# At most three indirect transfers in flight, in place of a wait for all at every fourth

## Time and profile before

| | us |
|---|---|
| median of three executions | 1523.4 |
| lowest, highest | 1520.61, 1532.26 |
| the profiled execution | 1523.45 |
| its span, first to last instruction | 1521.7 |
| PE busy (matmul) | 1223.2 (80% of the span) |
| DVE busy | 934.8 (61%) |
| POOL busy | 563.9 (37%) |
| ACT busy | 541.5 (36%) |

### The profile page before, as it was taken

The page is one execution under the profiler, slowest core; times in us unless marked ns, Lnnn a source line. Parts: engine busy times, 40 slices in busy tenths (PEclk is TensorE's granted clock), DMA queues, the critical chain, the costliest instruction groups (busy, mean ns, idle before and its releaser), DMA issues. The chain is left out here.

```text
span 1521.7 us, 31374 instructions
## 1 busy us (share of the span) xinstructions
PE 1223.2 (80%) x11687; PEld 1053.5 (69%) x11687; DVE 934.8 (61%) x2307; ACT 541.5 (36%) x1254; POOL 563.9 (37%) x645
## 2 busy tenths in 40 slices
PE   7999997895747999689985674858589999998920
PEld 4555557684747999689883453645589999988920
DVE  4777764788615644355544766575559777877732
ACT  3444431354605555244442331422323233222200
POOL 5000002000375656555205550055502555555655
PEclk9999998998558999899997785668579999999965
DMA  8600000004013333233214210011112333333341
GB/s 322 248 1 1 1 0 8 1 1 127 9 52 103 119 114 112 86 101 107 79 57 109 76 41 3 1 40 40 38 49 80 109 105 106 109 97 96 91 144 55
DMA packets 93251, 115.49 MB, mean 76 GB/s; under 512 B 18294, under 2 KB 77553, under 8 KB 93105
## 3 DMA queue, kind: packets, MB, share of 16 engines
q1 hardware_dynamic: 72144, 62.73, 13.4%
q0 software_dynamic: 20960, 50.76, 10.4%
HBM read 53.01 MB, written 60.42 MB: 75 GB/s over the span
## 5 line engine op out<-in xcount | busy, mean ns | idle before, releaser
L1393 POOL DMA_INDIRECT sorted_rows<-s_normed,s_places x128 | 130.8, 1022 | 211.5 <-DVE s_places L1359 120.8
L1554 PE MATMUL g_bank<-weights,gx_hT 128*128 x1360 | 169.8, 279 | 0.4 <-ACT gx_hT L1582 0.2
L1469 POOL DMA_INDIRECT sx_fetch<-sorted_results,s_places x128 | 132.7, 1037 | 99.9 <-DMA sx_fetch<-sorted_results,s_places 68.4
L1393 POOL DMA_INDIRECT sorted_rows<-g_normed,g_places x128 | 131.8, 1029 | 95.8 <-DMA sorted_rows<-g_normed,g_places 40.0
L1469 POOL DMA_INDIRECT gx_fetch<-sorted_results,g_places x128 | 126.0, 984 | 102.2 <-DMA gx_fetch<-sorted_results,g_places 70.8
L1554 PEld LDWEIGHTS g_bank<-weights,gx_hT 128*128 128x128 f32 x1360 | 162.7, 196 | 1.2 <-issue 1.2
L1517 PE MATMUL s_bank<-sx_xT_high,sx_w_now 128*128 128x256 f32 (+1 forms) x510 | 152.1, 298 | 1.8 <-DVE sx_hT L1629 1.2
L1518 PE MATMUL s_bank<-sx_xT_low,sx_w_now 128*128 128x256 f32 (+1 forms) x510 | 144.3, 283 | 0.0
L1519 PE MATMUL s_bank<-sx_xT_high,sx_w_now 128*128 128x256 f32 (+1 forms) x510 | 144.3, 283 | 0.0
L1554 PE MATMUL s_bank<-weights,sx_hT 128*128 (+1 forms) x1020 | 132.6, 280 | 5.4 <-issue 3.9
L1582 ACT ACTIVATE gx_hT<-g_bank,gx_b_now 128x256 f32<-128x256 f32 x340 | 132.8, 481 | 3.0 <-PE g_bank L1554 3.0
(11 more groups left out here) (434 smaller groups left out, 2757.6 us busy)
## 6 DMA issues: line engine op xcount, KB each, us to landing
sorted_rows<-zeros POOLq DMA_DIRECT2D x29, 512.0 KB, 15.5
gx_xq<-sorted_rows SPq DMA_DIRECT2D x85, 128.0 KB, 2.1
sorted_results<-gx_yq SPq DMA_DIRECT2D x85, 128.0 KB, 1.9
sx_xq<-sorted_rows SPq DMA_DIRECT2D x85, 128.0 KB, 2.1
sorted_results<-sx_yq SPq DMA_DIRECT2D x85, 128.0 KB, 2.2
feats<-in_x SPq DMA_DIRECT2D x8, 512.0 KB, 7.8
out<-tokens SPq DMA_DIRECT2D x16, 256.0 KB, 3.8
g_raw_up<-in_L_ffn_W SPq DMA_DIRECT2D x1, 2048.0 KB, 9.5
```

What stands on the lines that cost most here:

```text
L1393: pool.indirect_dma_start(out=sorted_rows[g], out_offset=bass.IndirectOffsetOnAxis(ap=places[:, at, r:r + 1], axis=0), in_=normed[:, at, : ...
L1469: pool.indirect_dma_start(out=fetch[n % 2][:, i, r, :], out_offset=None, in_=self.sorted_results[g], in_offset=bass.IndirectOffsetOnAxis(a ...
L1554: done = pe.matmul(down[u % 2][:, P * k:P * k + C], hT[u % 2][0:width, i, P * k:P * k + P], self.w_down[0:width, bass.ds(e, 1), i, :].rear ...
```

## The change

The waits at every fourth transfer go. In their place stands a class `Flight` with three semaphores that go round: transfer k of a stage counts on semaphore k mod 3, and before transfer k is issued POOL waits until transfer k - 3, the last on that semaphore, has landed. This holds for sends and fetches of both expert stages, the first group of the GELU stage included. Whoever needs a whole group or part (SP before the first unit of a group, DVE before the first tile of a part and at the start of the window attention) waits for the counts of all three semaphores in place of one. All other waits and the order of all work stay.

```diff
-def send_group(pool, plan, g, normed, places, sorted_rows, sent, pauses=True):
-    for at in range(plan.first_tile[g], plan.first_tile[g + 1]):
-        for r in range(2):
-            pool.indirect_dma_start(...).then_inc(sent[g], 16)
-        if at % 2 == 1 and pauses:
-            pool.wait_ge(sent[g], (at + 1 - plan.first_tile[g]) * 2 * 16)
+FLIGHT = 3
+class Flight:
+    def __init__(self, t, name):
+        self.slots = [t.sem(f"{name}{i}") for i in range(FLIGHT)]
+    def slot(self, k):
+        return self.slots[k % FLIGHT]
+    def wait_landed(self, engine, end):
+        for i, slot in enumerate(self.slots):
+            engine.wait_ge(slot, 16 * len(range(i, end, FLIGHT)))
+def send_group(pool, plan, g, normed, places, sorted_rows, sent):
+    for k in range(2 * plan.first_tile[g], 2 * plan.first_tile[g + 1]):
+        at, r = k // 2, k % 2
+        if k >= FLIGHT:
+            pool.wait_ge(sent.slot(k), k // FLIGHT * 16)
+        pool.indirect_dma_start(...).then_inc(sent.slot(k), 16)
...
                     for r in range(2):
+                        k = (n * SEND + i) * 2 + r
+                        if k >= FLIGHT:
+                            pool.wait_ge(fetched.slot(k), k // FLIGHT * 16)
                         pool.indirect_dma_start(
                             out=fetch[n % 2][:, i, r, :], out_offset=None, in_=self.sorted_results[g],
...
-                            ).then_inc(fetched[n % 2], 16)
-                    if i % 2 == 1:
-                        pool.wait_ge(fetched[n % 2], (n // 2 * SEND + i + 1) * 2 * 16)
+                            ).then_inc(fetched.slot(k), 16)
...
-                sp.wait_ge(self.sent[g], 2 * plan.tiles[g] * 16)
+                self.sent.wait_landed(sp, 2 * plan.first_tile[g + 1])
...
-            dve.wait_ge(self.fetched[part % 2], (part // 2 + 1) * 2 * SEND * 16)
+            self.fetched.wait_landed(dve, (part + 1) * 2 * SEND)
...
-                send_group(pool, plan, 0, normed, places, group_rows, sent, pauses=False)
+                send_group(pool, plan, 0, normed, places, group_rows, sent)
```

More of the change, by code:

```diff
@@ L1386, in place_in_pieces @@
         steps.settle()
-def send_group(pool, plan, g, normed, places, sorted_rows, sent, pauses=True):
-    for at in range(plan.first_tile[g], plan.first_tile[g + 1]):
-        for r in range(2):
-            pool.indirect_dma_start(
-                out=sorted_rows[g], out_offset=bass.IndirectOffsetOnAxis(ap=places[:, at, r:r + 1], axis=0),
-                in_=normed[:, at, :], in_offset=None).then_inc(sent[g], 16)
-        if at % 2 == 1 and pauses:
-            pool.wait_ge(sent[g], (at + 1 - plan.first_tile[g]) * 2 * 16)
+FLIGHT = 3
[12 more added lines that the diff above has]
+            pool.wait_ge(sent.slot(k), k // FLIGHT * 16)
+        pool.indirect_dma_start(
+            out=sorted_rows[g], out_offset=bass.IndirectOffsetOnAxis(ap=places[:, at, r:r + 1], axis=0),
+            in_=normed[:, at, :], in_offset=None).then_inc(sent.slot(k), 16)
 class Units:
@@ L1440, in __init__ @@
         self.alone = 0 if kind.gelu else 1
-        self.fetched = [t.sem(f"{tag}fetched{i}") for i in range(2)]
+        self.fetched = Flight(t, f"{tag}fetched")
         self.x_loaded = [t.sem(f"{tag}x_loaded{i}") for i in range(4)]
@@ L2208, in vector @@
         if units:
-            for g, n in enumerate(units.plan.tiles):
-                dve.wait_ge(units.sent[g], 2 * n * 16)
+            units.sent.wait_landed(dve, 2 * TT)
         normalise(0)
@@ L2245, in gelu_and_first_half @@
         normed = t.sbuf("g_normed", [P, TT, C])
-        sent = [t.sem(f"gx_sent{g}") for g in range(plan.groups)]
+        sent = Flight(t, "gx_sent")
         room = t.sbuf("g_room", [P, 4 * HALF])
@@ L2511, in silu_and_second_half @@
         normed = t.sbuf("s_normed", [P, TT, C])
-        sent = [t.sem(f"sx_sent{g}") for g in range(plan.groups)]
+        sent = Flight(t, "sx_sent")
         with ExitStack() as routing:
```

## The result

The changed kernel takes 1448.2 us (median; 1443.58 to 1451.21), the kernel before 1522.3 beside it: a ratio of 0.9505, 95% interval 0.9458 to 0.9551. Predicted were 1446 us. The profiled execution took 1451.2 us, with a span of 1449.5, 72.2 less than before.

| stretch (how measured) | before | after | gain so far | gain of the stretch | predicted |
|---|---|---|---|---|---|
| GELU group 0 (last send) | 455.28 | 455.13 | 0.15 | 0 | 0 |
| GELU units (POOL's clearing after all stores) | 797.09 | 763.62 | 33.5 | 33.5 | 33 |
| first window attention (POOL's first work behind it) | 938.25 | 896.89 | 41.4 | 7.9 | 11 |
| second window, SiLU units, end (last fetch) | 1513.87 | 1441.48 | 72.4 | 31.0 | 33 |

A forecast was written before the change was run, and what follows sets the result against it. The prediction took POOL's indirect transfers, idling until each burst of four landed, to bound the kernel from the SiLU stage on. Gains of 33 + 11 + 33 = 77 us against 1523.45 gave 1446, range 1436 to 1476.

The forecast's parts named there:

- Period: Spacing of POOL's transfers after the change: issue plus 0.30 us gap limits, not landings; 1.34 us, between 1.25 and 1.64.
- 4.5 at most: Longest landing time of a transfer in us, giving a third of landing plus resuming of 1.5 us at the worst.
- signs of a wrong forecast: DVE still waiting for fetches in units, POOL gaps for landings of k - 3, or issues over 1.04 us on average.
- GELU group 0 at nothing: First group's sends in the GELU stage, newly given waits: no loss at the nearest row, 11 us lost at the upper end.
- GELU units, 33: GELU stage units: SP's wait for group 2 and DVE's waits for fetches go, leaving 3.44 us a unit; 33 us less.
- up to p of about 1.9: In the GELU units, DVE was to have no waits for fetches while a transfer's period stayed below about 1.9 us.
- First window, 11: First window attention: most of DVE's 15.2 us of waiting for fetched parts goes; 11 us less, at worst 5, at best 15.
- SiLU units and end, 33: SiLU units to last fetch: stalls go, part 12 starts at 1439.4, last fetch starts 32.9 us earlier; 33 us less.
- Fetches stay late: Rival: POOL's wait for earlier adds replaces the removed one, DVE's 28.3 us of waits stay; time 1498, chance 0.08.
- Slower: Rival: three transfers in steady flight land later than bursts, at SP's GELU group 2 wait and last fetches; 1668, chance 0.05.
- no effect: Rival: landings hold POOL at its present pace throughout; time 1523, chance 0.03.
- DVE slows the issue: Rival: POOL's issues in the units meet DVE's 0.87 us weight copies, period 1.95 us; gain 20, time 1503, chance 0.05.

The follow-up runs named there:

- sends alone: Changed kernel with only the sends three in flight, fetches keeping the wait at every fourth transfer; 1498.3 us, ratio 0.9841 to the kernel before.
- free sends: Changed kernel with sends not waiting for landings at all, on one semaphore a group, fetches still three at a time; 1448.7 us, ratio 0.9542.
- copy on ACT and early adds: Changed kernel with the copy of a SiLU unit's weights moved from DVE to ACT and SiLU adds begun two steps earlier; 1438.7 us, ratio 0.9472.

## Why the prediction was right

- **Period.** The issue limits it, as argued. It was 1.28 to 1.39 us where I took 1.34. A fixed gap of 0.30 us stands before nearly every issue, met wait or none. My "4.5 at most" for a landing left out the GELU fetches, for which that trace has no landings on record; they are where over half of the waiting lies now (17.5 of 33 us). Two of my own signs of a wrong forecast did come, both small: the issue is 1.07 to 1.08 us on average in the SiLU stage, not 1.04, and POOL does stand for landings of k - 3, 33 times for longer than the usual gap. So the last 32 fetches do not run quite without pause.
- **GELU group 0 at nothing.** The new waits never held it.
- **GELU units, 33.** Measured 33.5. The steps hold one by one: group 2 sent by 593 (592.5 worked out), fetches from 594.5 (595), no wait of SP, no wait of DVE, 3.44 us a unit to the end. The margin was smaller than I wrote, though: I had DVE free of waits "up to p of about 1.9", but DVE wants a part each 12 us, that is 8 fetches at 1.5, and where a part took 14.2 us, 1.77 a fetch (sends alone, parts 3 to 7), it waited for fetches, 14.2 us in all.
- **First window, 11.** This is the term that was too large: 7.9 here, and between the same two points 4.5 in the second trace of the same kernel and 10.0 with free sends, at granted clocks of 0.75, 0.72 and 0.78 (0.72 before). The fetch waits went as foreseen, 12.0 us of them against the 11; the step that failed is that what DVE no longer waits for fetches is gained. PE's own work is late next, by 3.8 us here and 5.6 in the second trace.
- **SiLU units and end, 33.** Measured 31.0, and 32.9 from the first unit's copy on. That part 12 came on time is in part luck: the first unit's copy came 1.9 us late, counted from the end of the first window, and undisturbed units cost 3.75 us, not 3.80, which over 28 of them gave 1.3 back. Part 12 started at 1398.41, which is 1439.8 with the 41.4 us gained until then put back, against 1439.4 worked out. The other 2 us are the period of the last 32 fetches, 1.39 in place of 1.34: landings of up to 4.1 us beside the stores of tokens, and one pause of 2.20 that nothing in the profile explains. Sends of this stage bound nothing once the fetches are quicker: alone they gave 2.1 us.
- **Rivals.** *Fetches stay late* fell: adds and fetches kept pace. *Slower* and *no effect* fell: three in steady flight land soon enough, and it takes a depth of two to see the landings hold POOL back. *DVE slows the issue* was right in mechanism and small in price: the means grew by some 45 ns where closer issues met more copies, and the copies cost 0.09 to 0.12 us of a mean issue (985 and 958 ns without). The 1.65 us issue was the sign, and I was wrong to take it for a single one: in the trace before, 24 of the 128 SiLU fetches took over 1.1 us to issue, and each of them met such a copy, which the mean of 1.04 hid. The Trainium skill, "SBUF — State Buffer", the box on DVE blocking DMA, has GpSimd unable to write descriptors while such a copy runs on DVE; the traces without the copy on DVE agree (985 and 958 ns, no fetch over 1.1 us). The shorter issues alone did not move the end here.

The sum, 77, came to 72.4: the window's 3 and the period's 2. The first window alone differs by 3.4 us between the changed kernel's two traces, so it is in part luck that 1446 met 1448.2 so closely.

## What to carry to other kernels

A wait for a whole burst leaves the issuing engine idle until its last transfer has landed, here 1.5 us for every four. A rolling limit costs next to nothing once its depth times the issue period, here 3 x 1.26 us, exceeds nearly all landings with the restart behind them, and a deeper one earned nothing that could be told. Size the depth by the late landings and the restart, not by the median landing alone. Gains on one queue count only up to what is late next: two halves of this change overlapped by 10 us in one stage, one added nothing to the other in the next, and 27 us taken off POOL's issues came back as waits.

## What the runs showed of the hardware

A lone indirect transfer of 128 rows of 512 bytes lands 2.3 us (send) or 2.5 us (fetch) after its issue at the median (one in flight), and POOL's next one starts some 0.28 us after that; one of a burst lands after 2.4 or 2.8.

DVE's copy of 128x1368 in 0.87 us lengthens POOL's issue when they meet (1.34 us in the mean for the 42 SiLU fetches of the changed kernel that met one, 0.957 for the others); ACT's copy of the same in 1.35 us does not (0.956, none over 1.1).

The second window attention, in which no kernel here differs, took 53.3 us in the trace of the changed kernel and 47.5 with the copy on ACT and early adds, which affects nothing so early. The stretches (PE, PEld, DVE, ACT, POOL busy, granted clock, DMA share, GB/s), of the one and of the other:

```profile
897.00:950.00 53.00, 36.69 (x258) 27.98 (x258) 36.00 (x144) 18.41 (x40) 1.42 (x9) 0.63 0.00 1
```

```profile
897.00:945.00 48.00, 30.56 (x258) 21.68 (x258) 36.25 (x143) 18.41 (x40) 1.53 (x9) 0.71 0.00 1
```

The same 258 matmuls take 36.69 us at a mean granted clock of 0.63 and 30.56 at 0.71, both between the two levels of 1.2 and 2.4 GHz. The changed kernel's own second trace took 50.6 us there, at 0.67. So executions scatter by 3 to 6 us in this part alone, and a late stage is better compared from its own first instruction than by total time.
